# Neighbour tokens of a small convolution: SBUF to SBUF transfers in place of products with shifted identities

## The reference, cut to what matters

```
def _ode_func(A, conv1_w, gn_g, gn_b, conv2_w, conv2_b):
    h = _conv1d(A[:, None, :], conv1_w)          # 1 -> 4 channels, 3 taps, zero padding
    hg = h.reshape(b, 2, 2, n)                    # group norm, two groups
    mu = hg.mean((2, 3), keepdims=True)
    var = hg.var((2, 3), keepdims=True)
    h = ((hg - mu) * lax.rsqrt(var + GN_EPS)).reshape(b, 4, n)
    h = jax.nn.relu(h * gn_g[None, :, None] + gn_b[None, :, None])
    y = _conv1d(h, conv2_w) + conv2_b[None, :, None]   # 4 -> 1 channels, 3 taps
    return y[:, 0, :]
...
A = A + 1.0 * _ode_func(A, ...)
weights = jax.nn.softmax(jax.nn.sigmoid(A), axis=1)
out_low = weights[..., None] * v * ch_w
```

## Time and profile before

| | |
|---|---|
| median of 3 runs | 833.81 us (833.12 to 833.93) |
| profiled execution, its own time | 832.9 us |
| its span in the profile | 831.6 us |
| PE busy | 749.8 us, 90% |
| DVE busy | 701.7 us, 84% |
| ACT busy | 662.1 us, 80% |
| chain that ended last | PE 63%, ACT 16%, issue 9%, DVE 5% |
| TensorE's granted clock, mean | 0.962 of full |

### The profile page before, as it was taken

The page is one execution under the profiler, slowest core; times in us unless marked ns, Lnnn a source line. Parts: engine busy times, 40 slices in busy tenths (PEclk is TensorE's granted clock), DMA queues, the critical chain, the costliest instruction groups (busy, mean ns, idle before and its releaser), DMA issues.

```text
span 831.6 us, 18563 instructions
## 1 busy us (share of the span) xinstructions
PE 749.8 (90%) x5485; PEld 597.5 (72%) x5485; DVE 701.7 (84%) x2072; ACT 662.1 (80%) x1457; POOL 340.9 (41%) x370
## 2 busy tenths in 40 slices
PE   2789999999999999999999999999675999988872
PEld 1468777787877878888787887887543777777762
DVE  4867877899889889889988988988757799999885
ACT  2456668987997987898799798796744899999994
POOL 3000020133524224243342522337635299886767
PEclk9969999999999999999999999999868999999997
DMA  7113210202222131131213220102114458765430
GB/s 258 27 54 100 76 52 26 84 26 78 71 89 96 53 102 59 55 130 39 78 65 96 90 77 33 51 27 71 58 46 140 122 164 233 211 182 163 148 119 30
DMA packets 50306, 76.50 MB, mean 92 GB/s; under 512 B 8541, under 2 KB 31007, under 8 KB 50208
## 3 DMA queue, kind: packets, MB, share of 16 engines
q1 hardware_dynamic: 39104, 48.42, 20.0%
q0 software_dynamic: 9600, 25.25, 8.4%
q10 hardware_dynamic: 1504, 1.64, 0.6%
HBM read 47.42 MB, written 28.91 MB: 92 GB/s over the span
## 4 chain that ended last, share of the span: by engine, by line
PE 63%; ACT 16%; issue 9%; DVE 5%; POOL 4%; ACTq 1%; DMA 0%; DVEq 0%; POOLq 0%; SPq 0%
PE bank L592 8%; ACT G_S L1904 6%; PE bank L799 6%; PE bank L812 6%; PE bank L672 4%; ACT G_y L1920 3%; PE bank L544 3%; PE bank L674 3%; PE bank L673 3%; PE bank L684 3%; PE bank L620 2%; PE bank L621 2%; ACT G_T L1880 2%; PE bank L604 2%; PE bank L767 2%
## 5 line engine op out<-in xcount | busy, mean ns | idle before, releaser
L3462 POOL TENSOR_TENSOR R<-rstd,mhalf 128x4 f32<-128x4 f32 x16 | 19.5, 1220 | 278.8 <-DVE rstd L1961 278.8
L3633 POOL DMA_INDIRECT out<-G_y,Gid x72 | 83.6, 1161 | 35.4 <-ACT G_y L1920 13.2
L1904 ACT ACTIVATE G_S<-bank,e1b,e1s 128x256 f32<-128x256 f32 (+1 forms) x188 | 95.1, 651 | 2.2 <-PE bank L1285 2.2
L1285 PE MATMUL bank<-G_T,E1T 128*128 128x256 f16 (+1 forms) x752 | 76.4, 251 | 8.0 <-issue 4.4
L592 PE MATMUL bank<-X,PT 128*128 128x257 f32 x320 | 81.0, 392 | 1.1 <-DVE X L2005 0.9
L3506 POOL DMA_INDIRECT rrec<-R,pos x64 | 67.0, 1047 | 29.2 <-issue 20.7
L3497 POOL DMA_INDIRECT hrec<-HN,pos x64 | 65.7, 1027 | 29.0 <-issue 16.0
L1297 PE MATMUL bank<-E2T,G_Sh 128*128 x288 | 65.6, 274 | 9.5 <-DVE G_Sl L3437 9.2
L1285 PEld LDWEIGHTS bank<-G_T,E1T 128*128 x752 | 59.7, 99 | 19.6 <-issue 11.6
L812 PE MATMUL bank<-E2T,Sh 128*128 128x256 f16 x256 | 60.8, 282 | 6.3 <-DVE Sl L2138 6.3
L1297 PE MATMUL bank<-E2T,G_Sl 128*128 x288 | 65.8, 275 | 0.0
(11 more groups left out here) (392 smaller groups left out, 2459.2 us busy)
## 6 DMA issues: line engine op xcount, KB each, us to landing
XT<-in_xT SPq DMA_DIRECT2D x16, 512.0 KB, 3.9
X<-in_x SPq DMA_DIRECT2D x16, 512.0 KB, 5.8
G_h<-hrec SPq DMA_DIRECT2D x25, 257.0 KB, 3.6
G_r<-rrec SPq DMA_DIRECT2D x25, 257.0 KB, 3.5
e1n<-in_ew SPq DMA_DIRECT2D x8, 512.0 KB
e2n<-in_ew SPq DMA_DIRECT2D x8, 512.0 KB, 3.4
G_h<-hrec SPq DMA_DIRECT2D x22, 128.5 KB, 2.1
G_r<-rrec SPq DMA_DIRECT2D x22, 128.5 KB, 2.3
```

What stands on the lines that cost most here:

```text
L1285: last = pe.matmul(bk[:, o + a:o + b], E1T[:, e, c, ff * P:(ff + 1) * P], gt[:, x, c, a:b], start=k == 0, stop=k == 3)
L1904: last = act.activation(G_S[w % NGS][:, ff, a:b], bk[:, o + a:o + b], ACT.Silu, bias=e1b[:, e, ff], scale=e1s[:, e, ff])
L3633: pool.indirect_dma_start(t["out"], bass.IndirectOffsetOnAxis(Gid[w % NGI][:, j:j + 1], 0), G_y[w % NGY][:, j, :], None, bounds_check=TOK ...
```

## The change

The five products of `nb` and the five of `nb2` go. In their place SP issues, for each convolution, six transfers from SBUF to SBUF (`neighbours`): the bulk of the partitions one down and one up, split at 112 partitions, and one transfer for each partition end. `A` is written once into the middle of a new tile `o_N` (previous, own, next), and step 8 reads all three from there. For the second convolution the transfers go from `o_t` into a new tile `o_M`, whose middle is written by a new step 20 (own tap sum + bias + A); a new step 21 sums the three. So the chain has 28 steps. Both transfers are waited for in full: `near1` and `near2` have to reach 96 (six transfers of 16) more for each group. The tiles are padded, so that a partition's run is 16 floats.

Epsilon is now added by POOL in an instruction of its own ahead of the power, and `gn2` is one product. The four shift matrices go. On DVE, step 8 moves behind `Sl(2g-3,1)`, `Ml(2g-1)` and `one0(g-1,3)`, and the steps from 21 on move back, as the rows further down show.

```
     o_ds = sb("o_ds", [P, 2, GC, 2])
...
-    o_A = sb("o_A", [P, GB, CH, NT])
+    o_N = sb("o_N", [P, TAPS, GB, 2 * NT])
+    o_M = sb("o_M", [P, TAPS, GB, 2 * NT])
...
+        def neighbours(to, prev, nxt, sem):
+            sp.dma_start(to[1:PH + 1, 0], prev[0:PH]).then_inc(sem, 16)
+            sp.dma_start(to[0:PH, 2], nxt[1:PH + 1]).then_inc(sem, 16)
+            sp.dma_start(to[PH + 1:P, 0], prev[PH:P - 1]).then_inc(sem, 16)
+            sp.dma_start(to[PH:P - 1, 2], nxt[PH + 1:P]).then_inc(sem, 16)
+            sp.dma_start(to[0:1, 0, :, 1:NT], prev[P - 1:P, :, 0:NT - 1]).then_inc(sem, 16)
+            sp.dma_start(to[P - 1:P, 2, :, 0:NT - 1], nxt[0:1, :, 1:NT]).then_inc(sem, 16)
+        def near1(g):
+            sp.wait_ge(s["ode"], NO * g + 8)
+            neighbours(o_N, o_N[:, 1], o_N[:, 1], s["near1"])
+        def near2(g):
+            sp.wait_ge(s["ode"], NO * g + 20)
+            neighbours(o_M, o_t[:, 0], o_t[:, 2], s["near2"])
...
             load_x(2 * g - 1)
             load_x(2 * g)
+            near1(g - 2)
+            near2(g - 2)
             one_e2(g - 2)
...
-        def nb(g):
...
-            pe.matmul(taps[0], from_prev[:], A_tok, start=True, stop=False)
...
-            pe.matmul(banks[2][:, 0:GW], onesN[:], epsx[:], start=True, stop=False)
-            pe.matmul(banks[2][:, 0:GW], onesN[:], sq_flat, start=False, stop=True).then_inc(s["gn2"], 1)
+            pe.matmul(banks[2][:, 0:GW], onesN[:], sq_flat, start=True, stop=True).then_inc(s["gn2"], 1)
...
             elif k == 8:
-                dve.wait_ge(s["nb"], g + 1)
...
+                dve.wait_ge(s["near1"], 96 * (g + 1))
...
             elif k == 20:
-                dve.wait_ge(s["nb2"], g + 1)
-                ins = dve.scalar_tensor_tensor(o_e[:], bk[:, 0:GC].rearrange("p (b j) -> p b j", b=GB), c2b[:], A_one, ALU.add, ALU.add)
+                ins = dve.scalar_tensor_tensor(o_M[:, 1, :, 0:NT], o_t[:, 1, :, 0:NT], c2b[:], A_one, ALU.add, ALU.add)
             elif k == 21:
+                dve.wait_ge(s["near2"], 96 * (g + 1))
+                ins = dve.tensor_reduce(o_e[:], o_M[:, :, :, 0:NT].rearrange("p t b j -> p b j t"), AX.X, ALU.add)
...
             pool.wait_ge(s["ode"], NO * g + 14)
+            pool.tensor_scalar(o_rs[:], o_rs[:], 1e-5, None, ALU.add).then_inc(s["gnv"], 1)
+            pool.wait_ge(s["gnv"], g + 1)
             pool.tensor_tensor(o_rs[:], o_rs[:], mhalf[:, 0:2 * GB], ALU.pow).then_inc(s["gnr"], 1)
```

More of the change, by code:

```diff
@@ L364, in program @@
     sq_flat = o_sq[:].rearrange("p b c j -> p (b c j)")
-    A_flat = o_A[:].rearrange("p b c j -> p (b c j)")
-    A_one = o_A[:, :, 0, :]
-    NO = 27
+    A_one = o_N[:, 1, :, 0:NT]
+    NO = 28
+    PH = P // 8 * 7
     def sp_program():
@@ L468, in sp_program @@
         load_x(15)
-        one_e1(7)
+        near1(6)
+        near2(6)
         one_e2(6)
-        one_e2(7)
+        near1(7)
+        near2(7)
         def gload(w):
@@ L701, in u, with gn1 @@
             last.then_inc(s["u"], 1)
-        taps = [banks[2][:, k * GW:(k + 1) * GW].rearrange("p (n j) -> p n j", j=NT) for k in range(TAPS)]
-        A_tok = o_A[:].rearrange("p b c j -> p (b c) j")
-        def nb(g):
+        def gn1(g):
             if not 0 <= g < B // GB:
                 return
-            pe.wait_ge(s["ode"], NO * g + 8)
+            pe.wait_ge(s["ode"], NO * g + 10)
             if g >= 1:
@@ L1039, in pe_program @@
         x2T(2, 0)
-        nb2(0)
         pv(3, 2)
@@ L1148, in pe_program @@
             pv(2 * g + 1, 1)
-            nb2(g - 1)
             if g == 0:
@@ L1216, in pe_program @@
         u(15, 0)
-        nb2(7)
         u(15, 1)
@@ L2529, in rest @@
             elif k == 30:
-                ins = dve.memset(epsx[:], 1e-5)
+                dve.memset(o_N[:], 0.0)
+                dve.memset(o_t[:], 0.0)
+                ins = dve.memset(o_M[:], 0.0)
             elif k == 31:
@@ L2778, in dve_program @@
         ode(0, 19)
+        ode(0, 20)
         x1(3, 0)
@@ L2782, in dve_program @@
         x1(3, 1)
-        ode(0, 20)
+        ode(0, 21)
         guard(0, 6)
-        ode(0, 21)
+        ode(0, 22)
         TTl_(2, 0)
-        ode(0, 22)
+        ode(0, 23)
         guard(0, 7)
-        ode(0, 23)
+        ode(0, 24)
         rinv(3, 2)
         bn0(3, 0)
-        ode(0, 24)
+        ode(0, 25)
         one0(0, 5)
@@ L2798, in dve_program @@
         guard(0, 8)
-        ode(0, 25)
+        ode(0, 26)
         rinv(3, 3)
-        ode(0, 26)
+        ode(0, 27)
         x1(3, 3)
@@ L3115, in dve_program @@
             ode(g - 1, 19)
+            ode(g - 1, 20)
             TTl_(2 * g, 0)
@@ L3141, in dve_program @@
                 sort(6)
-            ode(g - 1, 25)
+            ode(g - 1, 26)
             rinv(2 * g + 1, 3)
@@ L3284, in dve_program @@
         place(13, 1)
-        for i in range(17, 20):
+        for i in range(17, 21):
             ode(7, i)
@@ L3288, in dve_program @@
         place(13, 2)
-        for i in range(20, 24):
+        for i in range(21, 25):
             ode(7, i)
         acc(13)
-        ode(7, 24)
+        ode(7, 25)
         Sl_(13, 3)
-        ode(7, 25)
         ode(7, 26)
+        ode(7, 27)
         for i in range(4):
@@ L3514, in pool_program @@
         for m, v in ((ident, 0.0), (ident16, 0.0), (identb, 0.0), (maskb, 0.0), (maskbT, 0.0), (ones, 1.0), (onesb, 1.0),
-                     (before, 0.0), (from_prev, 0.0), (from_next, 0.0), (edge_prev, 0.0), (edge_next, 0.0),
-                     (mhalf, -0.5)):
+                     (before, 0.0), (mhalf, -0.5)):
             pool.memset(m[:], v)
@@ L3520, in pool_program @@
         step(ins)
-        for m, base in ((ident, 0), (ident16, 0), (identb, 0), (from_prev, 1), (from_next, -1),
-                        (edge_prev, -(P - 1)), (edge_next, P - 1)):
+        for m, base in ((ident, 0), (ident16, 0), (identb, 0)):
             pool.affine_select(out=m[:], in_=m[:], compare_op=ALU.not_equal, fill=1.0, base=base,
```

77 lines of the change are left out of this document (27 added, 50 removed), and 2 rows, old and new, of the table names.

## The result

The changed kernel takes **913.08 us** (median of 4 runs, 911.01 to 914.36) against 833.87 us of the kernel before on the same chip (4 runs, 833.12 to 834.81). The ratio is **1.0952**, 95% interval 1.0932 to 1.0971: 79 us slower, where I had forecast 40. The direction was right, the size was not.

What follows compares the result with a forecast made beforehand. The prediction took PE, full in the loop turns of groups 1 to 6, as the bound. It summed 832.9 + 21.6 (loop) + 6.4 (group 0) + 6.6 (group 7) + 6.8 (clock) to 874 us, range 853 to 893.

Steps and rivals of the forecast that it cites:

- What bounds the kernel, and where it stalls: In the loop PE is full, 69.8 of 69.8 us; new idles come at `gn1`, the transposition and `osum`.
- The clock: After PE's 16 idles of 2.4 us or more, one in four lowers the clock: 4 x 1.7 = 6.8 us.
- every idle drops the clock: Rival for PE's idles: 16 clock falls in place of 4, 20 us more, 894; chance 0.08 with slow transfers, over 893.
- signs of being wrong: Six issues well under 2 us or landing within 1.5; more slack in DVE's order; clock falling much more or less often.
- The trip: From DVE's write through six SP issues, 0.47 us each, to the last landing, 2.2 us: 4.6 us in all.
- The legs at full clock: Groups 1 to 6: PE idles 2.6, 0.9 and 2.4 us, less 2.3 of work: +3.6 each, 21.6 us.
- Leg two: From `gn1` to the transposition behind `nb2`: PE idles 0.9 us there and is 1.2 late.
- The work removed: On PE, `nb` 1.03 us, `nb2` 1.12 and one `gn2` product 0.2 go: 2.3 us a group.
- Epsilon: POOL's extra addition takes 0.2 us, mostly under `x2p`; half of the power's shift shows, put in as 0.2.
- the rival of fast transfers: Trip 2.3 to 2.6 us, DVE's new order stays: loop 4 us, groups 0 and 7 5 us, 842 us; chance 0.10.
- Groups 0 and 7: Little DVE work covers the trip there; each convolution's step gap becomes 4.6 us: 6.4 and 6.6 us more.
- The sum: Whole kernel: 832.9 + 21.6 + 6.4 + 6.6 + 6.8 = 874.3 us, forecast as 874, 4.8% slower.

## Why the forecast had the direction and not the size

**What bounds the kernel, and where it stalls.** Right. PE is the bound, and it waits at the three places named, for the releasers named.

**The clock: of the single terms this one missed by most.** "I count one in four: 4 x 1.7 = 6.8 us." In groups 1 to 6 eleven of twelve idles brought it down, with 2.8 us missing from each (31 us / 11) and not 1.7. Filling the idles gave back 24.6 us. I had priced one idle by itself, and with one idle in a turn that is what is seen (0.76 over 7 us is 1.7 us). With two idles of 2.6 us and more, 16 us apart, most falls last twice as long. My rival "every idle drops the clock" used the same 1.7 us and ended at 894. That the clock falls much more often than one time in four was among the signs of being wrong that I had named.

**The trip: 4.6 forecast, 5.4 measured.** The landing was shorter (1.6, not 2.2), the six issues were longer: starts 0.76 us apart on average, not 0.47. The rows I took were of loads from HBM. The two errors partly cancelled, which was luck. My 2 us of turn for each us of trip was right (2.1 measured), so 0.8 us is 1.7 us a turn.

**The legs at full clock.** Forecast 2.6, 0.9 and 2.4 idle, less 2.3 of work: +3.6 a turn. This step failed too. With the clock held up: 7.6 us of PE's turn (75.72 - 68.14) are standing or filler, and 1.7 of work is gone: +5.9. Leg two was forecast 0.9 and is 1.7. Part of this is the trip, part the 1.1 us more on POOL, for which I had put 0.2. The work removed: 0.21 us a product forecast (2.3 for eleven), 0.22 measured where PE stays full, and yet only 1.7 for the eleven of the change. I think that each wait also uncovers the end of the product ahead of it; that is argued, not shown.

**Epsilon: priced at next to nothing.** I had POOL's extra addition at 0.2 us, mostly passing under `x2p`. The duration is one at 5.9 us of the span, far from these DVE instructions. `x2p` was not its cover but its obstacle. With epsilon's part alone the addition takes 1.73 us; in the changed kernel it takes 0.59, and the power behind it 1.86 in place of 1.41, so DVE waits 1.0 us at step 14. Alone the part costs 12.3 us. In the whole change taking it out gave nothing back: the idle at the transposition fell by 2.9 us in all, and the clock was lower. So no run shows a share of it in the 38 us that I missed. I expect that it would come out with faster transfers, but no run took it out of those.

**DVE's order.** I had 4 us for the loop in the rival of fast transfers; alone it costs 7.2. That rival as a whole, 842, was near: two transfers gave 848.

**Groups 0 and 7.** Forecast 6.4 and 6.6. In the filled version 9.9 (group 0, where an idle of 4.0 us at the transposition wasn't filled and the clock of the 7 us behind it read 0.64) and 7.1.

**The sum.** Measured 79.2. The clock is at least 24.6, against 6.8; the waits at full clock are at most 54.7, against 34.6. The first difference is 18, the second 20, and together they are the 38 us missing (79.2 against the 41.4 that the sum adds). Of the 20, the trip accounts for about 10 in the loop, by the 2.1 us above; how the rest is divided between DVE's order and POOL's two instructions stays open, since these overlap and don't add. Sharing the six issues between two queues, which might shorten the row, wasn't tried.

## What to carry to other kernels

On an engine that is full, a product taken out is worth its own 0.22 us and an in-order wait put in costs itself and then the clock behind it, so work out the longest dependent chain before counting the work saved. Price a stall with its clock by how it repeats (here a fall behind two idles in a turn mostly lasted twice as long as behind one), and a small instruction on POOL by what DVE runs beside it. Parts of a change measured alone don't add up within it: 12 us alone were 0 under larger waits.
